# Attention values matmul: the low half of the probabilities multiplies 66 of the 130 columns of latents

## The reference, cut to what matters

```
kv_up = _rms_norm(kv_c, kv_norm_w) @ wkv_b.T        # kv_c: 64 latents a token
scores = (einsum(q_nope, k_nope) + einsum(q_pe, k_pe)) * scale
scores = where(causal, scores, min)
probs = softmax(scores)
out = einsum('bhst,bthd->bshd', probs, v)           # v is a linear map of the latents
```

## Time and profile before

| | |
|---|---|
| time, median of 3 runs | 1614.83 us (1613.89 to 1616.1) |
| span of the profiled execution | 1608.3 us |
| median less span | 6.5 us |
| TensorE busy | 1528.2 us, 95% |
| `values` matmuls (L1090) | 4608, busy 307.9 us |
| granted TensorE clock, mean | 0.989 |

### The profile page before, as it was taken

One profiled execution on the slowest core, in us unless ns is written; L12 is line 12 of the kernel. 1 busy time (PEld: TensorE's weight loads), 2 busy tenths in 40 slices (PEclk: granted clock), 3 DMA queues, 4 the chain that ended last, 5 costly groups with the idle time before them and its releaser, 6 DMA issues.

```text
span 1608.3 us, 30457 instructions
## 1 busy us (share of the span) xinstructions
PE 1528.2 (95%) x10720; PEld 1278.0 (79%) x10720; DVE 1103.5 (69%) x2509; ACT 1121.8 (70%) x2207; POOL 954.8 (59%) x913
## 2 busy tenths in 40 slices
PE   6978999999999999999999999999978999999997
PEld 5866788888788888887888888888866778888875
DVE  6976777888787778887788888888875332323344
ACT  5777888878888887887888888888866553221144
POOL 2666867778677777776877878778722221111134
PEclk9999999999999999999999999999998999999999
DMA  8779999999999999999999999999988001101022
GB/s 278 258 164 209 189 209 194 207 210 185 205 191 205 187 205 204 189 212 202 186 198 193 184 197 184 200 193 186 190 220 294 27 27 40 40 1 41 1 79 105
DMA packets 661096, 268.85 MB, mean 167 GB/s; under 512 B 608432, under 2 KB 619184, under 8 KB 658768
## 3 DMA queue, kind: packets, MB, share of 16 engines
q1 hardware_dynamic: 660944, 266.90, 78.8%
HBM read 69.70 MB, written 29.36 MB: 62 GB/s over the span
## 4 chain that ended last, share of the span: by engine, by line
PE 73%; DMA 7%; DVE 6%; POOL 5%; ACT 4%; SPq 3%; issue 3%; POOLq 0%; ACTq 0%; DVEq 0%
PE s_ps L1076 20%; PE x_ps L163 16%; PE f_ps L163 13%; PE o_ps L1090 12%; PE fd_ps L163 6%; DMA qs<-q_raw 5%; PE x_ps L1099 1%; POOL qf L1680 1%; SPq L877 1%; POOL qs L1677 1%; POOL q_low L1687 1%; DMA pt<-pk 1%; PE x_ps L1107 1%; PE f_ps L1034 1%; PE a_ps L163 1%
## 5 line engine op out<-in xcount | busy, mean ns | idle before, releaser
L1521 DVE SCALAR_TENSOR_TENSOR pk<-s_ps,pk 128x512 f16<-128x512 f32 (+7 forms) x512 | 380.7, 752 | 119.1 <-ACT pk L1293 117.8
L1285 ACT ACTIVATE s_ps<-s_ps,nbias 128x512 f32<-128x512 f32 (+7 forms) x512 | 364.6, 719 | 61.7 <-DVE nbias L1508 57.7
L1508 DVE CUSTOM_DVE_ANT_0 s_ps<-s_ps,far_sb 128x512 f32<-128x512 f32 (+7 forms) x512 | 385.7, 761 | 29.2 <-PE s_ps L1076 28.4
L1293 ACT ACTIVATE pk<-s_ps 128x512 f16<-128x512 f32 (+7 forms) x512 | 327.3, 655 | 19.5 <-DMA pt<-pk 11.2
L1090 PEld LDWEIGHTS o_ps<-lat,pt 128*128 128x128 f16 x4608 | 266.7, 97 | 66.4 <-issue 61.5
L1090 PE MATMUL o_ps<-lat,pt 128*128 128x130 f16 x4608 | 307.9, 220 | 9.0 <-ACT o_norm L1302 6.4
L1076 PE MATMUL s_ps<-k_high,q_high 128*128 128x512 f32 (+3 forms) x768 | 285.2, 371 | 17.6 <-POOL q_low L1687 9.4
L1677 POOL TENSOR_TENSOR qs<-qs,sin_q 64x512 f32<-64x512 f32 x128 | 164.4, 1285 | 185.4 <-DMA qs<-q_raw 180.1
L1076 PE MATMUL s_ps<-k_low,q_high 128*128 128x512 f32 (+3 forms) x768 | 257.3, 342 | 0.0
L1718 POOL TENSOR_TENSOR mid_low<-mid,mid_high 128x512 fp32r<-128x512 f32 (+1 forms) x44 | 56.8, 1290 | 296.5 <-ACT mid_high L1382 296.5
L1076 PE MATMUL s_ps<-k_high,q_low 128*128 128x512 f32 (+3 forms) x768 | 220.8, 341 | 0.0
(11 more groups left out here) (142 smaller groups left out, 2614.1 us busy)
## 6 DMA issues: line engine op xcount, KB each, us to landing
weff_in<-weff SPq DMA_DIRECT2D x64, 256.0 KB, 3.4
qs<-q_raw SPq DMA_DIRECT2D x256, 64.0 KB, 2.6
weff<-weff_sb SPq DMA_DIRECT2D x8, 1024.0 KB, 5.3
wo_sb<-wo SPq DMA_DIRECT2D x16, 512.0 KB, 4.9
m_fold<-m_in SPq DMA_DIRECT2D x8, 1024.0 KB, 7.4
m_in<-m_fold SPq DMA_DIRECT2D x8, 1024.0 KB, 6.4
xin<-x SPq DMA_DIRECT2D x16, 256.0 KB, 4.4
wqn_sb<-wqn SPq DMA_DIRECT2D x8, 512.0 KB, 6.1
```

What stands on the lines that cost most here:

```text
L1285: e.activation(M.scores_of(i), M.scores_of(i), ACT.Exp, bias=M.nbias[:, i % 4:i % 4 + 1], scale=-1.0).then_inc(S.exp)
L1293: e.activation(M.halves_of(i)[:, :, 0, :], M.tiles_of(i), ACT.Copy, scale=P_SCALE).then_inc(S.p_high)
L1508: e.tensor_tensor_reduce(out=s, in0=s, in1=M.far_sb[:, SEQ - width:SEQ], scale=1.0, scalar=3e38, op0=ALU.add, op1=ALU.min, accum_out=M.nbi ...
L1521: e.scalar_tensor_tensor(out=M.halves_of(i)[:, :, 1, :], in0=M.tiles_of(i), scalar=P_SCALE, in1=M.halves_of(i)[:, :, 0, :], op0=ALU.mult, ...
```

## The change

In `values` the matmuls on a high half of probabilities still move all 130 columns. Those on a low half move 66: the high latents and the two ones. The product of low probabilities and low latents is no longer computed. So that the 66 columns stand side by side, `lat2` is laid out as low, high, ones; POOL's two instructions in `halves` write the same amounts to swapped places. `outputs_add` adds the two 64 column halves whichever comes first. No instruction is added, removed or moved, and no wait changes: there are 4608 matmuls and 4608 weight loads as before, and 2304 of the matmuls are 66 instead of 130 columns wide.

```diff
             for m in blocks:
-                ins = e.matmul(M.o_ps[:, i % 2, :], M.pt[:, u % NPT, m, :],
-                               M.lat2[:, b * JT + (m - blocks[0]) // 2, :], start=m == blocks[0],
+                t, low = divmod(m - blocks[0], 2)
+                side = slice(KVL, LATW) if low else slice(0, LATW)
+                ins = e.matmul(M.o_ps[:, i % 2, side], M.pt[:, u % NPT, m, :],
+                               M.lat2[:, b * JT + t, side], start=m == blocks[0],
                                stop=m == blocks[-1])
...
-        e.tensor_copy(M.lat2[:, i, 0:KVL], M.kl[:, r, :]).then_inc(S.lat_high)
+        e.tensor_copy(M.lat2[:, i, KVL:P], M.kl[:, r, :]).then_inc(S.lat_high)
         w.wait_ge(S.lat_high, i + 1)
-        e.tensor_tensor(M.lat2[:, i, KVL:P], M.kl[:, r, :], M.lat2[:, i, 0:KVL], ALU.subtract
+        e.tensor_tensor(M.lat2[:, i, 0:KVL], M.kl[:, r, :], M.lat2[:, i, KVL:P], ALU.subtract
                         ).then_inc(S.lat)
```

## The result

The changed kernel takes 1606.03 us (median of 12 runs, 1596.23 to 1611.17) against 1614.36 us (12 runs): a ratio of 0.9948, 95% interval 0.9932 to 0.9963. That is 8.3 us faster, where 32.9 were forecast and 61.4 were to be taken out of TensorE's work. The median lies just above the forecast's range, which ended at 1606, and the gain is a quarter of the forecast. The mean granted clock differs between these runs: in ten of them it is 0.982 to 0.985, at 1603.49 to 1611.17 us, and in the two others 0.988 and 0.989, at 1598.71 and 1596.23 us.

What follows compares the result with a forecast made beforehand. The prediction took TensorE to bound attention. A 61.4 us saving, less 21.9 us for the next head's queries and 6.6 us for SyncE's queue, gave 32.9 us: from 1614.8 to about 1582 us, range 1560 to 1606.

Steps and rivals of the forecast that it cites:

- What bounds the kernel now: In attention TensorE bounds: a microsecond taken from it is worth up to a microsecond if nothing else becomes late.
- What a values matmul costs: In `values`, columns set the pace: 57.7 ns between starts at 130 columns, 31 ns at 66, saving 26.7 ns.
- The first rival: In `values`, a weight load and its matmul keep 57.7 ns, so the time stays 1614.8 us; chance 0.08.
- The direct saving: In `values`, 2304 narrow matmuls save 26.7 ns each, 61.4 us, 0.96 us a head.
- the two losses: Waits taken off the saving: 21.9 us for the next head's queries and 6.6 us for SyncE's queue.
- other waits: `values` after `outputs_norm`, `scores` after `split_low`, and ScalarE's work: set at nothing, 5 us as the worse end.
- The queries of the next head: TensorE waits at `scores` for POOL's `q_low`, chain of eleven microseconds: loss 21.9 us, bounds 12 and 40.
- And SyncE's queue: Swaps stand behind transposes more often in shorter heads: 0.2 us at 33 heads, 6.6 us, between nothing and 33.
- the sum: Over the whole kernel, 61.4 - 21.9 - 6.6 = 32.9 us gained, to about 1582 us.
- stated signs of being wrong: TensorE's wait for `q_low` doesn't grow from 10.7 us, or a wait for transposes or `outputs_norm` takes its place.
- The third rival: The chain of queries bounds all heads, SyncE's queue being near full: gain some 8 us, 1607 us; chance 0.07.
- the slower rival: In attention, more waiting drops TensorE's clock to 1.2 GHz: 1629 us with three such heads, 1661 with five; chance 0.05.

Runs made afterwards that it cites:

- half transposes: Each pair's transpose takes only 9 of its 18 tiles, each used twice: 1597.74 us on the kernel before, 1559.76 us on the changed kernel.
- POOL's work cut: POOL's multiplication by the sine left out of `queries_turn`: 1609.48 us on the kernel before, 1602.81 us on the changed kernel.
- added issues: A 256 byte transfer added behind every second transpose in SyncE's queue, 128 in all: 1678.74 us on the kernel before, 1680.38 us on the changed kernel.

## Why the prediction was wrong

**What bounds the kernel now** was read half. The chain of the kernel before ran over TensorE, and rightly so: it was the bound. What the busy shares don't show, SyncE being no row of them, is a second bound right beside it, with 34.4 us of room over 63 heads, 0.55 us a head, where the change was to take 0.96.

**What a values matmul costs** was right. 18 matmuls last 0.96 us, the number forecast, and their starts lie 45.4 ns apart in the mean, where 9 at 57.7 and 8 at 31 give 45.1. The first rival, that the pair keeps its 57.7 ns, is refuted by these rows. The Trainium skill's 62 ns per MATMUL ("TensorE: Matmul & The Clock Gate", "Wait — 56ns, not 53.3ns?") holds, by that section, where decoding in hardware is off; the rows don't show such a limit in this kernel.

**The direct saving** of 61.4 us is the first step that failed, with what it took for granted: that all of it comes through but for the two losses. With half transposes the queue has 472 and more than 400 us of room, the wait for `q_low` is 0.7 us in the changed kernel, the clock is 1.00, and the change brings 38 us. The two traces tell where the rest is. I take each matmul from its start to the start of the next, less idle time, from the first to the last `values` matmul. `values` takes 260.6 us before and 207.3 after, 53.3 less and not 61.4: the narrow matmul in the last place of each block is hidden (256 x 26.7 ns would be 6.8 us). The other matmuls take 11.1 us more, most of it where a queries piece begins (6.4 us) and at the matmul just before a `values` block (3.6); TensorE's idle time grows by 2.6. That leaves 39.6 us, and the stretch is 39.5 us shorter. Why those other matmuls take longer no run here separates; the prediction had set all such effects, as **other waits**, at nothing.

**The queries of the next head**: the wait was to grow by 21.9 us, at 25 to 35 heads; it grew by 22.0 to 32.7, 28 times. The size came out and the reason didn't. The prediction set POOL's unbroken eleven microseconds against a shorter head. With half transposes POOL's work is the same and the head shorter still, and the wait is 0.7 us, 2 times; with POOL's work cut the wait fell to 7.3 us and the time by 3 us only. So the agreement of the number is luck in good part: the wait grew because the swaps came late out of a full queue.

**And SyncE's queue** is the step that failed in the mechanism. I had its rows and added them up to "over 14 of 16.7 us", by medians, took the rest for room, and sized the loss at 0.2 us for each of 33 heads, 6.6 us. The transposes take 3.1 us in the mean where the median is 2.84; the earlier trace rows had shown three in 9.59 us. By the records, a head of 16.7 us holds 15.5 us of issues and 0.6 us between them, and 0.55 us are free. Measured by the pair with half transposes against the pair as it is, the queue takes 38 - 8 = 30 us of the change. This contains the growth of the wait for queries, so it stands against both losses of the sum, 21.9 + 6.6 = 28.5 us, and not against the 6.6 alone. Together the two were sized well, with the queue's share put down to POOL; the 24.6 us by which the sum was off are nearly all in the 61.4 us, of which 38 come through. The queue also acts at a place that I had set at nothing: transposed pairs came late for TensorE (4.5 to 14.1 us) and `pk` for ScalarE (11.2 to 23.2). A wait for the transposes was one of the stated signs of being wrong, and it came, beside the one for the queries.

The same count of the two kernels as they are closes too. `values` takes 51.6 us less. TensorE's idle time grows by 27.8 us, of which 20.0 stand before scores (the queries) and 7.7 before `values` (the transposes and `outputs_norm`). The other matmuls take 15.1 us more, up to 5.1 of it by the clock. That leaves 8.7 us, by which the stretch is shorter.

The third rival (a gain of 8 us, 1607), which had 0.07, named the outcome, but not by its road: not all heads hung on the chain of queries, TensorE waited for it 28 times.

**The clock**, the slower rival, is there in small. Its mean from the first to the last `values` matmul is 0.995 where it was 1.00, which is 5.1 us of full clock, and the two runs of the changed kernel with a higher clock were the shortest, by 5 to 15 us. A lower clock and more waiting come together in these runs; which of them makes the other, no run separates.

## What to carry to other kernels

An engine that only issues transfers has no busy share here, so add up its queue like any other: count times mean duration, not median, plus the 0.09 us between two issues, against the period, and see how much of the rest is really free. When the bound engine gets faster, expect little more than the next resource has room for. Two losses with one cause behind them don't add up: measure them together, and measure what the saving is worth with the suspected resource relieved, which here was 38 us of 61. An experiment that adds a little load to a suspected queue is as telling as one that removes some: here 74 us of issues cost 63 us, and the gain of the change went to zero. Look at the granted clock beside each such run, since it moved too. Before moving an issue to another engine, price it there at the same 0.58 us.

## What was not expected of the hardware

An f16 matmul of 66 columns with its own weight load of 128 columns is followed by the next start after 29 ns in the median, and 18 alternating ones lie 45.4 ns apart in the mean. A transfer of 256 bytes occupies the issuing queue as long as one of 64 KB, 0.58 us in both on SyncE; one of the 128 KB of a whole swap took 0.47. Issues on ScalarE (64 KB, 0.56 us) and POOL (256 KB, 0.58 us) cost about the same there. A transpose's issue follows its size, 2.84 us for 18 tiles and 1.31 for 9. And the granted clock was lower in kernels where TensorE stood idle longer: from the first to the last `values` matmul it was 1.00 with 28.7 us of idle time (before), 0.995 with 56.5 (changed), 0.984 with 70.1 (added issues, before), 0.976 with 87.1 (low matmuls left out) and 0.966 with 100.2 (added issues, changed).
